# Context keys and values of ten batches made in the quantised layer and kept in DRAM; multi-query mask added by VectorE

## What is computed

```
L0_attn   multi-query attention, 8 heads of 128, one key/value head, causal
L0_xattn  attention to the context, 16 heads of 8, causal
L0_ffn    mixture of 8 experts, top 2
L1_attn   attention in windows of 64 with a position bias;  L1_xattn;  L1_ffn (linear experts)
L2_attn   rotary attention, causal;  L2_xattn  context attention, 16 heads of 64
L2_ffn    gated layer, weights in 4 bits, five tensors rounded to 16 bits by their global maximum
L3_attn   rotary attention, causal
L3_xattn  16 heads of 64; 256 keys per batch: 128 of the context and 128 of x itself
L3_ffn    512 wide, weights dequantised from int32
```

```
c  = layernorm(context) * g1 + b1          # depends on the inputs alone
h  = layernorm(x) * g2 + b2
q  = h @ Wq;  k, v = concat(c, h) @ Wkv    # 256 keys and values, 16 heads of 64
out = softmax(q @ k.T / 8 + key mask) @ v @ Wout
```

## Time and profile before

| | us |
|---|---|
| median of 3 runs | 1820.0 (1819.06 to 1822.94) |
| the profiled execution, its own time | 1822.76 |
| its span, first to last instruction | 1820.9 |
| outside the span | 1.9 |

### The profile page before, as it was taken

How to read it: one execution, slowest core, us unless ns; L and a number is a source line. 1 busy time by engine, 2 the same in 40 slices (tenths; PEclk the granted TensorE clock), 3 DMA queues, 4 the chain that set the end, 5 groups by cost and what they waited for, 6 DMA issues and landing times. The chain is left out here.

```text
span 1820.9 us, 41780 instructions
## 1 busy us (share of the span) xinstructions
PE 1662.0 (91%) x14797; PEld 1219.6 (67%) x14797; DVE 1427.3 (78%) x3951; ACT 1214.0 (67%) x4785; POOL 739.1 (41%) x926
## 2 busy tenths in 40 slices
PE   8999999999989998789999997628889999999998
PEld 7886568999755565246678886325556766667667
DVE  5667887778798988988857776888997777777765
ACT  3447996665799995159954443627986666666676
POOL 2225871000366883147720000026774434434446
PEclk9999999999876997799999999769999999999999
DMA  9000000000000000000000000200000000000000
GB/s 295 4 1 2 2 2 2 1 2 2 1 2 2 2 2 1 1 1 2 2 1 2 2 2 20 94 0 1 2 2 1 1 1 1 1 1 1 1 1 25
DMA packets 11678, 22.28 MB, mean 12 GB/s; under 512 B 5200, under 2 KB 8528, under 8 KB 10832
## 3 DMA queue, kind: packets, MB, share of 16 engines
q1 hardware_dynamic: 11472, 19.61, 3.4%
HBM read 18.55 MB, written 1.05 MB: 11 GB/s over the span
## 5 line engine op out<-in xcount | busy, mean ns | idle before, releaser
L1716 POOL TENSOR_TENSOR a_probs<-a_probs,a_rinv 128x512 f32<-128x512 f32 (+1 forms) x288 | 272.3, 947 | 177.8 <-DVE a_rinv L1549 174.2
L1339 ACT ACTIVATE a_probs<-bank,a_negmax 128x128 f32<-128x128 f32 x896 | 326.2, 438 | 18.9 <-DVE a_negmax L1518 18.8
L1716 POOL TENSOR_TENSOR c_probs<-c_probs,c_rinv 128x512 f32<-128x512 f32 x192 | 200.3, 1044 | 209.0 <-DVE c_rinv L1549 205.8
L1752 POOL TENSOR_TENSOR a_rstd<-a_ve,neg_half 128x1 f32<-128x1 f32 x128 | 70.4, 550 | 501.3 <-DVE a_ve L1607 500.5
L1339 ACT ACTIVATION_READ_ACCUMULATOR a_probs<-bank,a_negmax 128x1 f32 x896 | 240.4, 278 | 0.0
L1136 PEld LDWEIGHTS bank<-const,a_probs 128*128 128x128 f32 x1024 | 118.4, 147 | 113.5 <-issue 92.3
L1136 PE MATMUL bank<-const,a_probs 128*128 128x128 f32 x1024 | 178.6, 294 | 0.2
L1518 DVE TENSOR_REDUCE a_negmax<-bank 128x4 f32<-128x512 f32 x224 | 152.1, 680 | 21.6 <-PE bank L1107 17.5
L1556 DVE COPY a_probs_t<-bank 128x512 f32<-128x512 f32 (+1 forms) x192 | 118.6, 618 | 26.4 <-PE bank L1136 26.0
L1118 PE MATMUL bank<-state_t,w_L_ffn 128*128 128x128 f32 x1024 | 136.1, 276 | 0.0
L1337 ACT ACTIVATE c_probs<-c_probs,c_negmax 128x256 f32<-128x256 f32 x256 | 127.0, 502 | 0.0
(11 more groups left out here) (273 smaller groups left out, 4395.2 us busy)
## 6 DMA issues: line engine op xcount, KB each, us to landing
w_L_ffn<-in_L_ffn SPq DMA_DIRECT2D x1, 3184.0 KB, 20.0
w_L_xattn<-in_L_xattn SPq DMA_DIRECT2D x1, 2050.0 KB, 8.5
w_L_attn<-in_L_attn SPq DMA_DIRECT2D x3, 512.0 KB, 5.6
w_L_xattn<-in_L_xattn SPq DMA_DIRECT2D x1, 1536.0 KB, 9.1
ctx_t<-in_ctxT SPq DMA_DIRECT2D x1, 1024.0 KB, 11.9
ctx<-in_ctx SPq DMA_DIRECT2D x1, 1024.0 KB, 11.7
out<-state SPq DMA_DIRECT2D x16, 64.0 KB, 1.6
state_t<-in_xT SPq DMA_DIRECT2D x1, 768.0 KB, 8.7
```

What stands on the lines that cost most here:

```text
L1339: op = act.activation(p, bank_of("scores", n)[:, j * width:(j + 1) * width], ACT.Exp, bias=negmax[:, n % PB, j:j + 1], accum_out=rsum[:, n ...
L1716: pool.tensor_tensor(p, p, along(rinv[:, n % PB, 0:heads], wide(kind) // heads), ALU.mult).then_inc(sems["norm_done"], 1)
```

## The change

1. **Context work leaves LOOP_C.** The context is loaded by SP in LOOP_A, into the place of L0_attn's weights (`first_pack`), once the 16 batches of L0_attn are normalised. Its layernorm (DVE, POOL) is done in LOOP_A, one batch in each batch of L2_xattn.
2. **In the quantised layer** PE also turns the 16 contexts (four banks) and ACT scales them into `KV`. For the last 10 batches (`AHEAD`) PE makes the context's part of the keys (two banks) and of the values (two banks), 40 "halves" in seven banks; ACT copies them into four staging places, and SP stores each batch's 1 MB to the DRAM tensor `kept_halves`.
3. **In L3_xattn** the projection "c" is gone for all batches. For the 10 batches k0 and k1 hold own keys only, v0 and v1 are gone, and SP loads the stored halves (two DMAs of 512 KB a batch) when the scores, then the values, of the batch two before are made. `KX` has the context's keys and the own keys in two blocks, and not chunk by chunk. Values and outputs of this layer come one slot later.
4. **Multi-query mask.** PE's mask matmul is gone; DVE adds the mask and takes the row maximum head by head (four `tensor_tensor_reduce`, which write the negated masked scores back to the bank and the negated maximum to `negmax`), and ACT's exponential scales by -1.

```diff
 EARLY = {
-    "h64m": [("c", 12, "act"), ("q0", 10, "act"), ("k0", 9, "dve"), ("k1", 8, "act"), ("q1", 7, "dve"), ("k2", 6, "act"), ("k3", 5, "dve"), ("v0", 4, "act"), ("v2", 3, "dve"), ("v1", 2, "act"), ("v3", 1, "dve")],
+    "h64m": [("q0", 10, "act"), ("k0", 9, "dve"), ("k1", 8, "act"), ("q1", 7, "dve"), ("k2", 6, "act"), ("k3", 5, "dve"), ("v0", 4, "act"), ("v2", 3, "dve"), ("v1", 2, "act"), ("v3", 1, "dve")],
...
-    "values": {"all": -1, "h8": -2, "h8p": -2, "h8r": -2, "h64c": 1},
+    "values": {"all": -1, "h8": -2, "h8p": -2, "h8r": -2, "h64c": 1, "h64m": -2},
...
-CONTEXT_LEAD = 20
+AHEAD = 10
+EARLY_AHEAD = [("q0", 11, "act"), ("k0", 9, "dve"), ("q1", 7, "dve"), ("k1", 5, "act"), ("v2", 3, "dve"), ("v3", 1, "act")]
...
-            if self.kind(s) == "h64m":
-                self.context.setdefault(self.first[s] - CONTEXT_LEAD, []).append(s)
+            if self.kind(s) == "h64c":
+                self.context.setdefault(self.first[s], []).append(s)
...
         load_more(sp)
+        for m in range(AHEAD):
+            sp.wait_ge(wide_taken, N_WIDE + 4 * m + 4)
+            sp.dma_start(kept_halves[m], slots[slot_of(m)]).then_inc(stored[slot_of(m)], 16)
+
+    HALVES_BY = (2, 12, 32) + (N_HALVES,)
...
+        def context_half(i):
+            b = G - AHEAD + i // 4
+            pe.wait_ge(wide_taken, N_WIDE + max(i - 6, 0))
+            if i % 4 < 2:
+                for j in range(4):
+                    mm = pe.matmul(half_bank(i)[:, j * P:(j + 1) * P], wide_k[:, 4 * (i % 4) + j, :], KV[:, b, 0, :], start=True, stop=True)
+            else:
+                c = cols_of["L3_xattn"]["Wv"][0] + 512 * (i % 4 - 2)
+                mm = pe.matmul(half_bank(i)[:, :], KV[:, b, 0, :], w["L3_xattn"][:, c:c + 512], start=True, stop=True)
+            mm.then_inc(wide_full, 1)
+
+        for i in range(HALVES_BY[1]):
+            context_half(i)
         spread_max(GATED)
-        pe.wait_ge(wide_taken, 4)
+        for i in range(HALVES_BY[1], N_HALVES):
+            context_half(i)
...
+        halves_taken(0, HALVES_BY[0])
+        act.wait_ge(scale_ready, UP + 1)
+        for c in range(FC):
+            rounded(FC + c, inv[:, UP:UP + 1]).then_inc(up_rounded, 1)
+        halves_taken(HALVES_BY[0], HALVES_BY[1])
         act.wait_ge(scale_ready, GATED + 1)
         for c in range(1, FC):
             rounded(c, inv[:, GATED:GATED + 1]).then_inc(gated_rounded, 1)
+        halves_taken(HALVES_BY[1], HALVES_BY[2])
         act.wait_ge(scale_ready, PROD + 1)
...
             load_given(sp, "mask_bk1", given["mask_bk1"])
+            sp.wait_ge(sems["x_ready"], G)
+            load_given(sp, "ctx", CX)
...
+                                sp.wait_ge(stored[slot_of(m)], stored_by(m + 1, slot_of(m)))
+                                sp.wait_ge(sems["scores_ready"], plan.count("scores", plan.last[s - 2]))
+                                sp.dma_start(KX[:, r, 0, :, :].rearrange("p c k -> p (c k)"), kept_halves[m][:, 0:1024]).then_inc(keys_in[r], 16)
+                                sp.wait_ge(sems["values_ready"], plan.count("values", plan.last[s - 2]))
+                                sp.dma_start(V64[:, r, 0, :], kept_halves[m][:, 1024:2048]).then_inc(values_in[r], 16)
...
+                            elif name[0] == "k" and plan.ahead(s):
+                                for j in range(4):
+                                    mm = pe.matmul(bank[:, j * S:(j + 1) * S], wide_k[:, 4 * i + j, :], KV[:, b, 1, :], start=True, stop=True)
...
-                        mask = plan.layer(s).mask
+                        mask = None if plan.masked_by_dve(s) else plan.layer(s).mask
...
+                            if plan.masked_by_dve(s):
+                                for j in range(heads):
+                                    op = dve.tensor_tensor_reduce(of[:, j, :], of[:, j, :], part(const, "const", "causal"), scale=-1.0, scalar=3.0e38, op0=ALU.add, op1=ALU.min,
+                                                                  accum_out=negmax[:, n % PB, j:j + 1])
+                                op.then_inc(sems["negmax_ready"], 1)
+                                return
```

More of the change, by code:

```diff
@@ L218, in closes, with masked_by_dve, ahead @@
         return i == 3 if self.kind(s) in H8 else i % 2 == 1 if self.kind(s) in ("h64c", "h64m") else True
+    def masked_by_dve(self, s):
+        return self.layer(s).mask == "causal" and self.layer(s).name in MASKED_BY_DVE
+    def ahead(self, s):
+        return self.kind(s) == "h64m" and self.steps[s][1] >= G - AHEAD
     def later(self, what, s):
@@ L287, in heads_view, with slot_of, stored_by @@
     return ap.rearrange("p (n k) -> p n k", n=n)
+def slot_of(m):
+    return m % 4 if m < 8 else 2 + m % 2
+def stored_by(m, k):
+    return 16 * sum(slot_of(t) == k for t in range(m))
 def over(ap, n):
@@ L366, in quantised_ffn, with half_bank @@
     wide_full, wide_taken, fc_ready = sem("wide_full"), sem("wide_taken"), kept["fc_ready"]
+    N_WIDE, N_HALVES = 8, 4 * AHEAD
+    slots = (xq[:, :, :].rearrange("p b d -> p (b d)"), xqt[:, :], stage[:, 1, :], stage[:, 0, :])
+    def half_bank(i):
+        return banks[i % 7]
     N_W, N_X, N_H = 3, 4, 24
@@ L689, in decoder_kernel @@
         XT = sb("state_t", [P, B, S])
+        first_pack = sb("first_pack", [P, sum(n for _, n in cols[LOOP_A[0].name].values())])
+        CX = first_pack[:, 0:G * D].rearrange("p (g d) -> p g d", g=G)
         first_in = {(name, k): sem(f"{name}_in{k}") for k in range(2) for name in ("xT", "x")}
@@ L708, in decoder_kernel @@
         near_in = sem("near_in")
+        keys_in, values_in = ([sem(f"{n}_in{k}") for k in range(2)] for n in ("keys", "values"))
         qkv_in, bias_in, table_in, tables_ready, ones_ready = (sem(n) for n in ("qkv_in", "bias_in", "table_in", "tables_ready", "ones_ready"))
@@ L875, in wide, with loaded, stage_free @@
                 return 4 * WINDOW if kind == "h8p" else 512
+            def loaded(s):
+                return 16 * sum(plan.ahead(t) and plan.ring(t, 2) == plan.ring(s, 2) for t in range(s + 1))
+            def stage_free(eng):
+                for k in range(2, 4):
+                    wait_once(eng, stored[k], stored_by(AHEAD, k))
             def attended(s, kind):
@@ L1042, in scores @@
                         bank = bank_of("scores", n)
+                        if last_loop and n == 0 + UNITS["down"] * G:
+                            ffn["halves_left"](pe)
                         bank_free("scores", n)
@@ L1283, in take @@
                             op = act.activation(QK[:, plan.ring(s, 2), 1, :], bank[:, S:2 * S], ACT.Identity, bias=W(s, "bk"))
-                        elif name == "c":
-                            if b == 0:
-                                act.wait_ge(w_in["L3_xattn"], 16)
-                            g, e = (part(w["L3_xattn"], "L3_xattn", k) for k in ("g1", "b1"))
-                            op = act.activation(KV[:, b, 0, :], bank[:, 0:S], ACT.Identity, scale=g, bias=e)
                         elif name == "gateT":
@@ L1292, in take @@
                             i = int(name[1])
-                            op = act.activation(KX[:, plan.ring(s, 2), 2 * i:2 * i + 2, :, :].rearrange("p c a k -> p (c a k)"), bank[:, :], ACT.Copy)
+                            if plan.ahead(s):
+                                op = act.activation(KX[:, plan.ring(s, 2), 1, 4 * i:4 * i + 4, :], heads_view(bank[:, :], 4), ACT.Copy)
+                            else:
+                                op = act.activation(KX[:, plan.ring(s, 2), :, 2 * i:2 * i + 2, :].rearrange("p o c k -> p c o k"), bank[:, :].rearrange("p (c o k) -> p c o k", c=2, o=2), ACT.Copy)
                         elif kind == "h64m" and name[0] == "q":
```

120 lines of the change are left out of this document (79 added, 41 removed).

## The result

The changed kernel took 1757.8 us (median of 4 runs, 1754.07 to 1758.91), the kernel before in the same rounds 1819.5. The ratio is 0.9656, 95% interval 0.9634 to 0.9677: 61.7 us less by the medians, where 46.7 were forecast. The profiled execution of after took 1754.07 by its own time (span 1752.2).

The account below looks back on a forecast made before the run. PE was taken to bound L0_attn and L3_xattn, DVE the rotary stage, with PE mostly idle in the quantised layer. Terms -41 - 2 + 0.5 + 1.8 - 1 - 5 = -46.7 from 1820.0 gave 1774 us, range 1762 to 1797.

Parts of the forecast that it names:

- L3_xattn: Cross-attention stage of 12 batches: 34 + 0.7 + 5.7, 41 us won, bounds 25 and 46.
- the term for PE's waits: L3_xattn: half of PE's 1.14 us of waits a batch won in ten batches, 5.7 us.
- The later slot for values costs nothing in itself: L3_xattn: moving values one slot later has no cost, as slots then hold scores or values, not both.
- this queue nearly empties: L3_xattn: 6 projections instead of 11 in the ten batches nearly empty the queue of the two use banks.
- rival 3: L3_xattn: PE, DVE and ACT in lockstep bring new waits, 25 us won for 41, 1790 in all; chance 0.12.
- The halves: L3_xattn: prepared keys save 1.6 and values 1.72 us a batch; with the turned context's 0.12, 3.4 together.
- Context layernorm: DVE's layernorm, some 0.9 us a batch: 2 us won in the rotary stage, 0.5 us lost in L2_xattn.
- Quantised layer: Spread maximum makes DVE 1.8 us late; full clock ahead of the down projection wins 1 us.
- Rival 2: Quantised layer: clock stays at half, 33 us lost throughout or some 20 for half the time, 1794; chance 0.11.
- Mask: L0_attn: moving the mask from PE to DVE nets -0.35 us a batch times 15 batches, 5 us won.
- rival 1: L0_attn: DVE's pairs run end to end, 14 us lost for 5 won, 1793 in all; chance 0.12.
- Rival 4: L3_xattn: reloads come late, the change turns slower from about 25 us to landing, 1873 at 30; chance 0.03.

Follow-up runs that it names:

- e4: The kernel before with only the later slot for values and outputs in L3_xattn: 1807.9 us, ratio 0.9926 to the kernel before.
- e6: The changed kernel with no halves prepared for any batch (AHEAD = 0 for 10): 1796.5 us, ratio 0.9879 to the kernel before.
- e3: The changed kernel with values and outputs of L3_xattn put back in their old slot: 1786.4 us, ratio 0.9808 to the kernel before.
- e9: The changed kernel with values in their old slot and the ten batches' six projections one slot earlier: 1758.1 us, ratio 0.9659 to the kernel before.
- e7: The changed kernel with DVE's context layernorm done once more at its old places: 1762.5 us, ratio 0.9701 to the kernel before.
- e11: The changed kernel with halves prepared for 13 batches instead of 10: 1756.3 us, ratio 0.9645 to the kernel before.

## Why the prediction was right or wrong

**L3_xattn, -41 forecast, -51.3 measured.** The step that failed is the term for PE's waits: "I count half of the wait as won: 0.57 x 10 = 5.7", and nothing of it in the six other batches, which "lose only the 0.12". Measured, all 1.14 us a batch went in the ten (11.4), and the period of the others fell by 0.77, which is 4.6 for six, where 0.7 was forecast. That is 9.6 of the 10.3 us missed. Two reasons stood behind the term. The first, lockstep of PE, DVE and ACT, kept half of the waits in the sum; in the changed kernel none came. The second was one sentence, "The later slot for values costs nothing in itself", with the slot then left out of the sum and not followed to the buffers. (DVE's 18.1 us less two copies of 0.7 and 0.9 is 15.8 and not 15.9; nothing hangs on it.)

What the slot does depends on what else is changed. Three kernels in a row give one account: the slot 9.9 (before to e4), the context turned elsewhere 0.8 (e4 to e6, 0.7 forecast), the halves 40.6 (e6 to after). e3 gives another: with all the rest in place the slot is worth 30.0, and nothing of that comes from the batches without prepared halves, where it costs 0.30 a batch. The wait ahead of the values projection goes by the slot alone (e4) and also without it (e3). So the forecast's reason, "this queue nearly empties", holds for the two use banks: e3 has one wait of 0.7 ahead of values and three of 0.4 ahead of the state left in 300 us. It looked at those two banks alone, counted a projection as only a cost, and did not see that projections also stood between two turns of one bank. "New waits in L3_xattn" was rival 3, at 25 us gained for 41: e3 is that case (21), with ACT's copy of the turns as the mechanism. The slot turned it away, and so does another order of the projections (e9, 48.1). That the change as forecast held this cure was luck.

**The halves.** 4.02 us a batch with the waits. The forecast was 3.4 by start to start and half of 1.14 besides, or 4.0: the right number for the wrong parts. The one wait that the halves remove over e6 is 0.4. Keys and values were priced at 0.87 and 0.86; in e6 the groups followed by scores or products take 0.96 and 0.95. A group's pitch depends on what comes behind it. Over two batches keys and values in e6 take 3.83 and 3.63 us a batch, in after 1.97 and 1.72: 3.8 us saved. The 0.4 us ahead of the transposed state goes too, and 0.15 comes back in gaps elsewhere. All of PE's waits were won, the end of the stated bounds (46), and the six other batches and the pitches carried it past that.

**Context layernorm, -2 forecast, -7.3 measured.** The place was right (DVE in the rotary stage), and the count too (three batches). The size failed: the work was priced, 0.9 a batch, and not what stands behind it. In e7 PE idles 3.4 us longer, mostly behind DVE, and works at half clock in two pieces (4.2 us more for the same work). In L2_xattn +0.5 was forecast and -0.3 measured; DVE has 112.61 us of work in 139.80 there and PE does not notice.

**Quantised layer, +0.8 forecast, +0.1 measured.** The details came as worked out: the first halves at half clock, full clock ahead of the down projection. ACT took "up" at 1169.99, 7.5 us before; less the 10.1 that after is ahead at this point, that is 2.6 late for 1.8. The spread maximum was 3.6 us late by the same measure (1.8 forecast), its use by DVE 2.2, the down projection 1.1, and the full clock gave that back by the first state. "It fits with nothing to spare" is what e11 shows: 12 halves more cost 12.0 us. Rival 2 (half clock throughout) fell: the halves keep PE at work, and the clock rose while they ran. In e6, without them, it was at half for 44.4 us.

**Mask, -5 forecast, -5.3 measured.** The number is right by two errors against each other. The pairs are 0.25 apart for 0.26, by the overlap read off, and rival 1 fell. Four of them take 0.95 us, inside their room of 1.06, which the forecast put just outside; so a steady batch wins 0.42 and not 0.35. But it was to be 15 such batches, "with full overlap", and it is twelve: the last three periods win 0.2 together. The Trainium skill's sentence that weighed against this (VectorE: DVE Perf Modes, section The DRAIN you can't avoid: the next operation does not start until the pipeline is empty) was read without the one that follows it in the same paragraph, that a next op which is not held starts earlier. The trace agrees with the second: pairs with 0.28 to 0.32 and 0.13 us of duration start every 0.25.

**Rival 4** (late reloads) fell: 4.4 us to landing, for 5.6 in the earlier trace rows, and no wait for them.

**Total.** -51.3 - 7.3 - 5.3 and about nothing in between are -63.9, against -61.7 by the medians; stages with a changing clock differ by up to 5 us from run to run, which can cover the rest. Of the 15 us missed, 10 are PE's waits in L3_xattn and 5 the delays behind the layernorm. The range's lower end, 1762, was to hold "all waits won and the pairs inside their room"; by the forecast's own terms that is 1774 - 5 - 2 = 1767, so it had 5 us over, and they did not reach for the waits won in the six other batches and the delays behind the layernorm.

## What to carry to other kernels

An edit that only reorders is not free until the row shows what it puts between two users of a single buffer: write down the new sequence on the bound engine for one period, and for each buffer ask what stands between two of its users. Removing work from the bound engine also removes cover; here the same halves were worth 0.7 or 4.0 us a batch (e3, after) by what else stood in the slot. Two edits that cure the same wait do not add up: ask what each is worth with the other in place. And price a step on an engine that others wait for by who is next in its row, not by its own duration.

## What the runs showed of the hardware

- Four VectorE pairs in a row (128 columns in PSUM, in place, and an accumulator read) cost 0.95 us, start to start, though their durations add up to 1.76 (after, 95.02 to 95.97 us).
- In the rotary stage the granted clock fell to the lower level (1.2 GHz) for some 3.4 us within 2 us of a wait of PE of 1.66 to 2.19 us: twice in before, twice in e7, once in e4, each of which has three such waits. The others (1.78 us at 1345 us in before, for one) were not followed so, and after, with no wait over 0.92 us there, has no such piece. So a wait of this length goes with the lower clock but does not always bring it, and nothing here isolates the rest of the cause.
- The time from the start to the first normalised batch differed by 3 us (34.5 to 37.4) between traces of kernels that are the same up to there, or nearly. A difference of that size early in a trace is no effect of a change.
- Ten stores of 1024 KB and the twenty reloads raised the DMA traffic from 22.28 to 43.28 MB. In the ten batches that is a DMA share of 0.15, and no engine waits for it.
